# Layer 2's queries projected straight into transposed form, two units at a time

## The chip, the cores and the metric

The kernel runs on one NeuronCore of a Trainium2 chip. Its engines work at the same time, each through its own list of instructions in program order, and meet by semaphores: TensorE (PE, matrix products; PEld is its loading of weights), VectorE (DVE), ScalarE (ACT), GpSimd (POOL) and SyncE (SP, which issues transfers). PE writes into PSUM, from where DVE and ACT take results to SBUF. The metric is the time of one execution on the device, in microseconds (us).

## The reference, cut to what matters

The input x is two batches of 1024 rows of 256 numbers. Four layers follow, each added to x: two attention layers and two mixtures of experts. The second attention layer, the one that is changed, is:

```python
xn = layernorm(x, g_in)
q = (xn @ Wq).reshape(b, n, H, DH).transpose(0, 2, 1, 3) * scale
kv = xn @ Wkv
k, v = (kv[..., :DH], kv[..., DH:])
...
sim = jnp.einsum('bhid,bjd->bhij', q, k)
sim = sim + bias
...
sim = jnp.where(causal_mask, neg, sim)
sim = jnp.where(mask_p[:, None, None, :], sim, neg)
attn = jax.nn.softmax(sim, axis=-1)
out = jnp.einsum('bhij,bjd->bhid', attn, v)
out = out.transpose(0, 2, 1, 3).reshape(b, n, INNER)
out = out @ Wo
return layernorm(out, g_out)
```

There are H = 16 heads of DH = 64, one key and value for all heads, and a null key and value in front. The first attention layer also normalizes each query and key row to length 1; the second does not.

## The kernel before

Attention goes over tiles of 128 query rows (8 a layer), and in a tile over 8 *units*: 4 groups of 4 heads, times 2 batches. A unit u has 4 *steps*, one per head. N = 512 steps n are written out in one list for both layers, m, k = divmod(n, 4). The tile number sets how many keys a step has (causal): 128 in a layer's first tile, 1024 in its last.

In step n, each engine has a fixed order of work that belongs to different units and steps:

- PE: the scores of step n + 3 (lines 1347 and 1348, queries stationary, keys moving); at k = 0 the output product y of unit m - 2; at k = 3 the transposes of the queries of unit m + 2 (line 1371); at k = 1 the projection of the queries of unit m + 3 (rows of x stationary, wq moving); then the transposes of the probabilities of step n (line 1456) and the product with the values of step n - 1. A function `small()` in the middle of a step holds the rest: for a new tile the transposes of x (xt, 15 steps ahead), keys and values (11 and 7 steps ahead); at k = 0 the null score of unit m + 1, at k = 2 the transposes of the attention output (o_n, line 1444).
- ACT: the exponential of step n + 1 (probs, line 673); at k = 0 the eviction of y (line 687); at k = 3 the evictions of the transposed queries to q_b (line 694, one for each of two halves of partitions) and a copy of q_b to q_a (line 698); at k = 1 the eviction of the projected queries to q_n (line 707); then p_hi of step n (line 765).
- DVE: at k = 1 the output of a unit (o_raw, r_den); the score pass of step n + 2 (line 994, which adds the bias, applies the mask and keeps the row's extreme); at k = 3 the rest of the queries to q_a (line 1022, two halves); then p_lo of step n (line 1078), with ot_lo (line 1068) or neg_null behind it at k = 2 and k = 0.

Numbers that PE multiplies are kept as a sum of two 16-bit halves, hi and lo, so each product is three (`three`, lines 1157 to 1159), and the queries stand in q_b (upper 64 partitions a constant for the mask, lower the hi half) and q_a (hi and lo), transposed, with two slots by u % 2. Each wait is written by hand, as in ACT's part at k = 3:

```python
act.wait_ge(s["q_t"], u + 1)
if u >= 2:
    act.wait_ge(s["scores"], HU * (u - 1))
```

PSUM has 8 banks: four for scores, two for transposed probabilities (tp), one for the output (op) and one, aux, for all else. While tiles have up to 512 keys, halves of the score banks are free, and `banks(n)` gives them to y and to `small()`; in wider tiles everything uses aux, and `take` makes PE wait until the last user of the bank has been read.

Of the kernel before, what the change touches and what calls it, by code (L numbers as in the profile page):

```python
# [28 lines left out]
P = 128  # L29
# [5 lines left out]
HU = 4  # L35
# [56 lines left out]
def model(nc, a, out):  # L92
# [3 lines left out]
    with ctx:  # L96
# [26 lines left out]
        q_n = sb("q_n", [P, 2, UW])  # L123
        q_sq = sb("q_sq", [P, HU, DH])
# [49 lines left out]
        ones64 = sb("ones64", [G, P])  # L174
# [72 lines left out]
        def sems(part, names):  # L247
# [8 lines left out]
                    q_proj q_sq q_ss q_nd q_na q_t q_hi q_lo q_dup q_null null  # L256
# [160 lines left out]
        def _(pool):  # L417
# [29 lines left out]
            gp.memset(q_b[DH:P, :, :], BIG).then_inc(setup["big"], 1)  # L447

# [4 lines left out]
            pool.wait_ge(setup["big"], 1)  # L453
# [140 lines left out]
        def _(act):  # L594
# [63 lines left out]
            for n in range(FIRST, LAST):  # L658
# [29 lines left out]
                if k == 3 and 0 <= m + 2 < NU:  # L688
# [10 lines left out]
                if k == 1 and 0 <= m + 3 < NU:  # L699
                    u = m + 3  # L700
                    act.wait_ge(s["q_proj"], u + 1)
                    if u < U0:
                        if u >= 1:
                            act.wait_ge(s["q_ss"], u)
                        ac.activation(q_sq[:, :, :].rearrange("p h d -> p (h d)"), first[:, 0:UW], ACT.Square)\
                            .then_inc(s["q_sq"], 1)
                    ac.activation(q_n[:, u % 2, :], first[:, 0:UW], ACT.Copy, scale=1.0 if u < U0 else DH ** -0.5 / WS)\
                        .then_inc(s["q_na"], 1)

                def small():  # L710

                    for T in range(STEPS):
                        n0 = T * STEP_N
                        layer, t = divmod(T, TILES)
                        if n == n0 - 15:
                            act.wait_ge(s["xt"], T + 1)
                            if T >= 2:
                                act.wait_ge(s["q_proj"], UNITS * (T - 1))
# [77 lines left out]
        def _(dve):  # L796
# [167 lines left out]
            for n in range(FIRST, LAST):  # L964
# [53 lines left out]
                if k == 3 and 0 <= m + 2 < NU:  # L1018
# [133 lines left out]
        def _(pe):  # L1152
# [165 lines left out]
            for n in range(FIRST, LAST):  # L1318
# [6 lines left out]
                if 0 <= i < N:  # L1325
# [6 lines left out]
                    if h == 0:  # L1332
                        pe.wait_ge(s["q_dup"], u + 1)
                        pe.wait_ge(s["q_lo"], 2 * (u + 1))
# [9 lines left out]
                    for c0 in range(0, w, 512):  # L1344
                        cw = min(512, w - c0)
                        o_ = sc[i % 2][:, c0:c0 + cw]
                        te.matmul(o_, q_a[:, u % 2, cols], k_a[layer][:, bt, c0:c0 + cw], start=True, stop=False)  # L1347
                        last = te.matmul(o_, q_b[:, u % 2, cols], k_b[layer][:, bt, c0:c0 + cw],  # L1348
# [15 lines left out]
                if k == 3 and 0 <= m + 2 < NU:  # L1364
# [3 lines left out]
                    if u < U0:  # L1368
                        pe.wait_ge(s["q_nd"], u + 1)
# [3 lines left out]
                if k == 1 and 0 <= m + 3 < NU:  # L1373
                    u = m + 3
                    layer = u // U0
                    T, hg, bt = u // UNITS, (u % UNITS) // B, u % B
                    take(False, (s["q_na"], u + 1), (s["q_sq"], min(u + 1, U0)))
                    if hg == 0:
                        if layer == 0:
                            pe.wait_ge(s["xr_lo"], T + 1)  # L1380
                        pe.wait_ge(s["xt_lo"], T + 1)
                        if T % TILES == 0:
                            pe.wait_ge(job_done, job_end[3 * layer + 1])
                    for kc in range(KC):
                        cols = slice(hg * UW, (hg + 1) * UW)
                        x_q = xr if layer == 0 else xt[:, T % 2]
                        last = three(first[:, 0:UW], x_q[:, 0, bt, kc, :], x_q[:, 1, bt, kc, :],
                                     wq[layer][:, 0, kc, cols], wq[layer][:, 1, kc, cols],
                                     kc == 0, kc == KC - 1)
                    last.then_inc(s["q_proj"], 1)  # L1390

                def small():
# [31 lines left out]
                    if k == 0 and 0 <= m + 1 < NU:  # L1424
# [4 lines left out]
                        pe.wait_ge(s["q_lo"], 2 * (u + 1))  # L1429
                        if u == 0:  # L1430
                            pe.wait_ge(setup["big"], 1)
# [66 lines left out]
```

## Time and profile before

| What | us |
|---|---|
| median of 3 runs | 1704.15 |
| their range | 1701.85 to 1704.22 |
| the profiled execution | 1700.64 |
| its span, first to last instruction | 1698.8 |

The profile is that of one execution; its span is the time from its first to its last instruction, and 1.8 us of the execution lie around it. Layer 1's steps go from 88.6 us to 740.8, layer 2's to about 1352, and the two mixtures of experts follow. A unit of queries is the same work in both layers, but for the normalization in layer 1 (a squaring on ACT, a sum on DVE, and a scaling on POOL).

### The profile page before, as it was taken

The page shows a single profiled execution, that of the slowest core. Times are in us where ns is not written, and L with a number is a line of the kernel's source. Part 1 is how long each engine was busy: PE and PEld are TensorE (multiplying, and loading weights), DVE is VectorE, ACT ScalarE, POOL GpSimd, SP SyncE. Part 2 cuts the span into 40 slices and gives each one's busy share as a digit, 9 for nine tenths or more (in the row PEclk, how much of TensorE's full clock was granted, in tenths as well). Part 3 has the DMA queues.
Part 4 walks back from the last instruction along what each step waited for, and adds up shares of the span by engine and source line. Part 5 has one row for each costly group of instructions (what it writes and reads, how often), then busy time and mean ns, then how long its engine had stood idle before and what let it go on. Part 6 is the DMA issues. An engine that isn't in the chain of part 4 may idle for free.

```text
span 1698.8 us, 46470 instructions
## 1 busy us (share of the span) xinstructions
PE 1458.5 (86%) x16377; PEld 1076.6 (63%) x16377; DVE 1415.3 (83%) x3651; ACT 1210.4 (71%) x3064; POOL 750.8 (44%) x1412
## 2 busy tenths in 40 slices
PE   1467778888889999987788888999999989999998
PEld 1245556666667777765666666677777756666665
DVE  4557778888898999987788888899999979888886
ACT  1268778888889989988888888889999923333332
POOL 5657776543433434356665332323212156632222
PEclk9679999999999999999999999999999999999999
DMA  4002121211122213111221211222123001000000
GB/s 140 5 27 63 52 63 51 81 65 43 66 76 88 88 51 126 57 39 32 70 76 58 76 64 70 76 82 71 63 101 131 22 1 43 2 1 1 14 14 26
DMA packets 50504, 96.70 MB, mean 57 GB/s; under 512 B 3396, under 2 KB 27092, under 8 KB 50276
## 3 DMA queue, kind: packets, MB, share of 16 engines
q1 hardware_dynamic: 45568, 90.27, 16.1%
q10 hardware_dynamic: 4708, 3.45, 0.7%
q8 instruction: 135, 2.21, 0.5%
q14 instruction: 93, 0.76, 0.1%
HBM read 91.54 MB, written 2.17 MB: 55 GB/s over the span
## 4 chain that ended last, share of the span: by engine, by line
PE 46%; DVE 18%; ACT 14%; issue 10%; POOL 3%; DMA 1%; DVEq 0%; ACTq 0%; POOLq 0%; SPq 0%
PE tp L1456 7%; DVE p_lo L1078 7%; ACT p_hi L765 6%; DVE biased L994 5%; PE sc L1159 4%; PE sc L1157 4%; PE sc L1158 4%; PE sc L1347 3%; ACT q_b L694 3%; PE sc L1348 3%; ACT probs L673 3%; PE op L1157 2%; PE aux L1157 2%; PE tp L1157 2%; PE tp L1159 2%
## 5 line engine op out<-in xcount | busy, mean ns | idle before, releaser
L1078 DVE TENSOR_TENSOR p_lo<-tp,p_hi 128x512 f16<-128x512 f32 (+3 forms) x768 | 416.7, 554 | 119.1 <-ACT p_hi L765 112.2
L994 DVE CUSTOM_DVE_ANT_0 biased<-sc,bias,neg_null 128x256 f32<-128x256 f32 (+7 forms) x512 | 411.2, 803 | 2.7 <-issue 0.8
L673 ACT ACTIVATE probs<-biased,neg_max 128x256 f32<-128x256 f32 (+7 forms) x512 | 395.7, 773 | 14.4 <-DVE neg_max L994 12.8
L1456 PE MATMUL tp<-ident,probs 128*128 128x128 f32 x2304 | 388.6, 278 | 17.5 <-DVE p_lo L1078 15.5
L765 ACT ACTIVATE p_hi<-tp 128x512 f16<-128x512 f32 (+3 forms) x768 | 368.9, 491 | 43.0 <-PE tp L1456 32.8
L1157 PE MATMUL op<-v_s,p_hi 128*128 128x64 f16 x2304 | 284.9, 194 | 53.9 <-DVE p_lo L1078 35.2
L1347 PE MATMUL sc<-k_a,q_a 128*128 128x512 f16 (+3 forms) x768 | 254.4, 331 | 67.0 <-DVE neg_max L994 59.9
L1456 PEld LDWEIGHTS tp<-ident,probs 128*128 128x128 f32 x2304 | 267.9, 142 | 52.3 <-issue 37.6
L1158 PE MATMUL op<-v_s,p_hi 128*128 128x64 f16 x2304 | 284.0, 194 | 0.0
L1159 PE MATMUL op<-v_s,p_lo 128*128 128x64 f16 x2304 | 284.0, 194 | 0.0
L1157 PEld LDWEIGHTS op<-v_s,p_hi 128*128 128x128 f16 x2304 | 215.8, 99 | 85.9 <-DVE p_lo L1078 62.2
L1348 PE MATMUL sc<-k_b,q_b 128*128 128x512 f16 (+3 forms) x768 | 242.0, 329 | 0.0
L1158 PEld LDWEIGHTS op<-v_s,p_hi 128*128 128x128 f16 x2304 | 210.2, 98 | 7.4
L1159 PEld LDWEIGHTS op<-v_s,p_lo 128*128 128x128 f16 x2304 | 210.5, 98 | 0.0
L477 POOL TENSOR_TENSOR p_lo<-probs,p_hi 128x512 f16<-128x512 f32 x80 | 92.5, 1156 | 176.2 <-ACT p_hi L650 176.2
L529 POOL TENSOR_TENSOR denom<-rows,p_null 128x4 f32<-128x4 f32 x128 | 25.6, 200 | 325.0 <-ACT p_null L774 325.0
L1347 PEld LDWEIGHTS sc<-k_a,q_a 128*128 128x128 f16 x768 | 75.2, 98 | 130.2 <-DVE neg_max L994 89.5
L497 POOL TENSOR_TENSOR o_n<-o_raw,r_den 128x256 f32<-128x256 f32 x128 | 78.4, 613 | 147.1 <-DVE o_raw L973 145.9
L650 ACT ACTIVATE p_hi<-probs 128x512 f16<-128x512 f32 x80 | 50.4, 630 | 130.5 <-DVE probs L926 130.5
L1022 DVE TENSOR_TENSOR q_a<-aux,q_b 64x256 f16<-64x256 f32 x256 | 108.1, 422 | 27.7 <-ACT q_b L694 20.0
L644 ACT ACTIVATE biased<-sc 128x512 f32<-128x512 f32 x80 | 47.7, 596 | 90.5 <-PE sc L1159 90.5
L694 ACT ACTIVATE q_b<-aux 64x256 f16<-64x256 f32 x256 | 96.5, 377 | 20.5 <-PE aux L1371 14.5
(268 smaller groups left out, 3609.7 us busy)
## 6 DMA issues: line engine op xcount, KB each, us to landing
bias<-rel_table SPq DMA_DIRECT2D x4, 2048.0 KB, 8.4
bias<-in_fside_16xSxS SPq DMA_DIRECT2D x4, 2048.0 KB, 8.0
bias<-rel_table SPq DMA_DIRECT2D x4, 1792.0 KB, 8.1
bias<-in_fside_16xSxS SPq DMA_DIRECT2D x4, 1792.0 KB, 7.1
bias<-rel_table SPq DMA_DIRECT2D x4, 1536.0 KB, 6.1
bias<-in_fside_16xSxS SPq DMA_DIRECT2D x4, 1536.0 KB, 6.6
bias<-rel_table SPq DMA_DIRECT2D x4, 1280.0 KB, 6.1
bias<-in_fside_16xSxS SPq DMA_DIRECT2D x4, 1280.0 KB, 5.6
```

The source lines that it names most:

```text
L673: ac.activation(probs[:, i % 2, 0:w], biased[:, i % 2, 0:w], ACT.Exp, bias=neg_max[:, u % 2, i % HU:i % HU + 1], scale=-1.0, accum_out=row ...
L694: ac.activation(heads(q_b[0:DH, u % 2, :], e), first[e * DH:(e + 1) * DH, 0:UW].rearrange("p (c q) -> p c q", q=P), ACT.Copy)\
L765: ac.activation(p_hi[:, gi % 4, 0:nb * P], tp[gi % 2][:, 0:nb * P], ACT.Copy)\
L994: ve.tensor_tensor_reduce(out=biased[:, i % 2, 0:w], in0=sc[i % 2][:, 0:w], in1=bias[:, g % 2, i % HU, 0:w], scale=-1.0, scalar=neg_null[: ...
L1022: ve.tensor_tensor(heads(q_a[DH:P, u % 2, :], e), first[e * DH:(e + 1) * DH, 0:UW].rearrange("p (c q) -> p c q", q=P), heads(q_b[0:DH, u % ...
L1078: ve.tensor_tensor(p_lo[:, gi % 4, 0:nb * P], tp[gi % 2][:, 0:nb * P], p_hi[:, gi % 4, 0:nb * P], ALU.subtract).then_inc(s["p_lo"], 1)
L1157: te.matmul(out_, l_hi, r_hi, start=first, stop=False)
L1158: te.matmul(out_, l_hi, r_lo, start=False, stop=False)
L1159: return te.matmul(out_, l_lo, r_hi, start=False, stop=last)
L1347: te.matmul(o_, q_a[:, u % 2, cols], k_a[layer][:, bt, c0:c0 + cw], start=True, stop=False)
L1348: last = te.matmul(o_, q_b[:, u % 2, cols], k_b[layer][:, bt, c0:c0 + cw], start=False, stop=True)
L1456: last = te.transpose(tp[gi % 2][:, jj * P:(jj + 1) * P], probs[:, n % 2, (j0 + jj) * P:(j0 + jj + 1) * P], ident[:, :])
```

## The change

For layer 2's units (u from U0 = 64 on) the projection is turned round: wq is stationary and x, for both batches, is moving, so the product comes out transposed, for two units at once (the same heads of both batches). It is done in the even unit's step k = 1, for units m + 2 and m + 3; ACT takes hi of both units to q_b in two instructions, DVE forms lo of both in two, and ACT's copies of hi to q_a follow at k = 2 and k = 3, one for each unit. Row-wise queries (q_n) and their transposes are gone there, and at k = 3 and in odd units at k = 1 the old work is left out. Queries get a second pair of buffers: q_a2 is the memory of q_n, q_b2 is new, and POOL fills its constant half in the set-up; for room, some small tiles of the set-up move into the memory of biased. Layer 1 works as before.

```diff
+        def q_pair(u):
+
+            return (q_a2, q_b2) if u // 2 % 2 == 0 else (q_a, q_b)
...
+        def q_parts(u):
+
+            return 2 * (u + 1) if u < NU // 2 else 2 * (u // 2 * 2 + 2)
...
+            gp.memset(q_b2[DH:P, :, :], BIG).then_inc(setup["big"], 1)
...
+                if k == 1 and U0 <= m + 2 < NU and m % 2 == 0:
+                    u = m + 2
+                    act.wait_ge(s["q_dir"], (u - U0) // 2 + 1)
+                    act.wait_ge(s["scores"], HU * (u - 2))
+                    for e in range(2):
+                        ac.activation(pair_heads(q_pair(u)[1][0:DH, :, :], e), pair_in(first, e), ACT.Copy,
+                                      scale=DH ** -0.5 / WS).then_inc(s["q_hi"], 2)
+                if k >= 2 and U0 <= m + 2 < NU and m % 2 == 0:
+                    u = m + k
+                    act.wait_ge(s["q_hi"], q_parts(u))
...
+                    ac.activation(q_of(u)[0][0:DH, :], q_of(u)[1][0:DH, :], ACT.Copy).then_inc(s["q_dup"], 1)
-                if k == 3 and 0 <= m + 2 < NU:
+                if k == 3 and 0 <= m + 2 < U0:
...
+                if k == 1 and U0 <= m + 2 < NU and m % 2 == 0:
+                    u = m + 2
+                    dve.wait_ge(s["q_hi"], q_parts(u))
...
+                    for e in range(2):
+                        ve.scalar_tensor_tensor(pair_heads(q_pair(u)[0][DH:P, :, :], e), pair_in(first, e),
+                                                DH ** -0.5 / WS, pair_heads(q_pair(u)[1][0:DH, :, :], e),
+                                                ALU.mult, ALU.subtract).then_inc(s["q_lo"], 2)
-                if k == 3 and 0 <= m + 2 < NU:
+                if k == 3 and 0 <= m + 2 < U0:
...
+                if k == 1 and U0 <= m + 2 < NU and m % 2 == 0:
                     u = m + 2
-                    take(False, (s["q_lo"], 2 * (u + 1)))
+                    T, hg = u // UNITS, (u % UNITS) // B
+                    take(False, (s["q_lo"], q_parts(u)))
...
+                    for c in range(UW // P):
+                        cols = slice(hg * UW + c * P, hg * UW + (c + 1) * P)
+                        for kc in range(KC):
+                            last = three(first.rearrange("p (b c q) -> p c b q", b=B, q=P)[:, c],
+                                         wq[1][:, 0, kc, cols], wq[1][:, 1, kc, cols],
+                                         xt[:, T % 2, 0, :, kc, :], xt[:, T % 2, 1, :, kc, :],
+                                         kc == 0, kc == KC - 1)
+                    last.then_inc(s["q_dir"], 1)
+                if k == 3 and 0 <= m + 2 < U0:
```

How the instructions stand on ACT, in layer 2's tile of 512 keys: before, from a unit's step k = 1 to its step k = 3 (a step begins with probs; q_n is the row-wise eviction, q_b and q_a the transposed queries).

```order
L673 ACTIVATE probs,rows<-biased,neg_max 128x512
L707 ACTIVATE q_n<-aux 128x256
L765 ACTIVATE p_hi<-tp 128x512
L673 ACTIVATE probs,rows<-biased,neg_max 128x512
L765 ACTIVATE p_hi<-tp 128x512
L754 ACTIVATE ot_hi<-sc 128x256
L673 ACTIVATE probs,rows<-biased,neg_max 128x512
L694 ACTIVATE q_b<-aux 64x2x128 x2
L698 ACTIVATE q_a<-q_b 64x512
L765 ACTIVATE p_hi<-tp 128x512
```

The same steps of an even unit after the change (here the buffer of q_a lies in the memory of q_n, and has its name).

```order
L697 ACTIVATE probs,rows<-biased,neg_max 128x512
L717 ACTIVATE q_b<-aux 64x4x128 x2
L802 ACTIVATE p_hi<-tp 128x512
L697 ACTIVATE probs,rows<-biased,neg_max 128x512
L724 ACTIVATE q_n<-q_b 64x512
L802 ACTIVATE p_hi<-tp 128x512
L791 ACTIVATE ot_hi<-sc 128x256
L697 ACTIVATE probs,rows<-biased,neg_max 128x512
L724 ACTIVATE q_n<-q_b 64x512
L802 ACTIVATE p_hi<-tp 128x512
```

The evictions of the transposed queries, now of 512 columns, have moved from k = 3 to k = 1, and one copy stands ahead of p_hi at k = 2 and at k = 3. In an odd unit none of these rows is there.

On DVE, the same tile, before: the steps k = 2 and k = 3 of a unit (a score pass is two rows, ISA).

```order
L994 ISA biased,neg_max<-sc,bias,neg_null 128x512
L994 ISA neg_max 128x1
L1078 TENSOR_TENSOR p_lo<-tp,p_hi 128x512
L1068 TENSOR_TENSOR ot_lo<-sc,ot_hi 128x256
L994 ISA biased,neg_max<-sc,bias,neg_null 128x512
L994 ISA neg_max 128x1
L1022 TENSOR_TENSOR q_a<-aux,q_b 64x2x128 x2
L1078 TENSOR_TENSOR p_lo<-tp,p_hi 128x512
```

After the change, from the step k = 1 of an even unit to its step k = 3.

```order
L1031 ISA biased,neg_max<-sc,bias,neg_null 128x512
L1031 ISA neg_max 128x1
L1061 SCALAR_TENSOR_TENSOR q_n<-aux,q_b 64x4x128 x2
L1124 TENSOR_TENSOR p_lo<-tp,p_hi 128x512
L1031 ISA biased,neg_max<-sc,bias,neg_null 128x512
L1031 ISA neg_max 128x1
L1124 TENSOR_TENSOR p_lo<-tp,p_hi 128x512
L1114 TENSOR_TENSOR ot_lo<-sc,ot_hi 128x256
L1031 ISA biased,neg_max<-sc,bias,neg_null 128x512
L1031 ISA neg_max 128x1
L1124 TENSOR_TENSOR p_lo<-tp,p_hi 128x512
```

The two subtractions have moved from k = 3 to k = 1 and have twice the columns; at k = 3 nothing stands between the score pass and p_lo.

## Rows read from the trace of the kernel before

**Rows 1.** the page, part 1: each engine, busy us (share), instructions.

```profile
PE 1458.5 (86%) x16377; PEld 1076.6 (63%) x16377; DVE 1415.3 (83%) x3651; ACT 1210.4 (71%) x3064; POOL 750.8 (44%) x1412
```

**Rows 2.** windows, two tiles of layer 2: busy us, instructions; clock, DMA share, GB/s.

```profile
915.90:987.70 71.80, 62.65 (x781) 47.88 (x780) 61.10 (x161) 61.55 (x159) 25.18 (x54) 1.00 0.22 68
...
1256.50:1345.00 88.50, 86.43 (x1184) 68.61 (x1183) 84.31 (x164) 80.93 (x164) 20.95 (x45) 1.00 0.28 96
```

**Rows 3.** DVE in time, a unit of 512 keys: start, us, instruction, [idle].

```profile
938.09 0.74 DVE L994 CUSTOM_DVE_ANT_0 biased<-sc,bias,neg_null 128x512 f32<-128x512 f32 x1
...
940.13 0.72 DVE L994 CUSTOM_DVE_ANT_0 biased<-sc,bias,neg_null 128x512 f32<-128x512 f32 x1
...
941.95 0.74 DVE L994 CUSTOM_DVE_ANT_0 biased<-sc,bias,neg_null 128x512 f32<-128x512 f32 x1
...
943.66 0.74 DVE L994 CUSTOM_DVE_ANT_0 biased<-sc,bias,neg_null 128x512 f32<-128x512 f32 x1
...
944.68 0.88 DVE L1022 TENSOR_TENSOR q_a<-aux,q_b 64x256 f16<-64x256 f32 x2 [0.28 <-ACT q_b L694]
945.97 0.69 DVE L1078 TENSOR_TENSOR p_lo<-tp,p_hi 128x512 f16<-128x512 f32 x1 [0.41 <-ACT p_hi L765]
946.58 0.74 DVE L994 CUSTOM_DVE_ANT_0 biased<-sc,bias,neg_null 128x512 f32<-128x512 f32 x1
```

**Rows 4.** ACT in time, the same unit, its step k = 3 on.

```profile
943.89 0.77 ACT L694 ACTIVATE q_b<-aux 64x256 f16<-64x256 f32 x2
944.68 0.63 ACT L698 ACTIVATE q_a<-q_b 64x512 f16<-64x512 f16 x1
945.34 0.60 ACT L765 ACTIVATE p_hi<-tp 128x512 f16<-128x512 f32 x1
...
946.63 0.37 ACT L687 ACTIVATE y_acc<-sc 128x256 f32<-128x256 f32 x1
```

**Rows 5.** PE in time, the same unit, its step k = 1.

```profile
938.99 0.38 PE L1347 MATMUL sc<-k_a,q_a 128*128 128x512 f16 x1
...
939.42 0.27 PE L1157 MATMUL aux<-wq,xt 128*128 128x256 f16 x1
...
939.96 0.27 PE L1159 MATMUL aux<-wq,xt 128*128 128x256 f16 x1
940.07 0.60 PE L1456 MATMUL tp<-ident,probs 128*128 128x128 f32 x4
```

**Rows 6.** instructions by form, layer 2: count, busy us, mean ns, idle before.

```profile
L1078 DVE TENSOR_TENSOR p_lo<-tp,p_hi 128x512 f16<-128x512 f32 x185 | 126.8, 689 | 34.4 <-ACT p_hi L765 32.4
L765 ACT ACTIVATE p_hi<-tp 128x512 f16<-128x512 f32 x186 | 110.3, 597 | 14.9 <-PE tp L1456 11.2
...
L1022 DVE TENSOR_TENSOR q_a<-aux,q_b 64x256 f16<-64x256 f32 x126 | 53.2, 422 | 12.2 <-ACT q_b L694 8.4
...
L694 ACT ACTIVATE q_b<-aux 64x256 f16<-64x256 f32 x126 | 47.4, 376 | 7.7 <-PE aux L1371 5.1
...
L1371 PE MATMUL aux<-ident,q_n 128*128 128x128 f32 x126 | 26.0, 289 | 3.9 <-DVE ot_lo L1068 3.3
...
L707 ACT ACTIVATE q_n<-aux 128x256 f32<-128x256 f32 x61 | 23.4, 384 | 27.4 <-PE aux L1159 26.7
```

**Rows 7.** waits of PE, us 1000 to 1340: us, times, longest.

```profile
PEld aux L1157 <- DVE q_a L1022: 10.8, 29, 1.2
PEld aux L1371 <- DVE ot_lo L1068: 10.3, 26, 0.6
```

**Rows 8.** line 994 over a 768-key tile, layer 1, then layer 2.

```profile
L994 DVE CUSTOM_DVE_ANT_0 biased<-sc,bias,neg_null x32: 981/1007/1019, 446.4 to 536.7; 128x768 f32<-128x768 f32 x32
...
L994 DVE CUSTOM_DVE_ANT_0 biased<-sc,bias,neg_null x32: 981/1007/1018, 1074.0 to 1160.7; 128x768 f32<-128x768 f32 x32
```

**Rows 9.** POOL in time, the start of the kernel.

```profile
19.89 0.95 POOL L447 MEMSET q_b<- 64x1024 f16 x1
...
55.42 0.28 POOL L440 TENSOR_SCALAR r_rs<-r_mv 128x8 f32<-128x8 f32 x1 [9.45 <-DVE r_mv L834]
```

More of the change, by code:

```diff
@@ L698, in _ @@
                     ac.activation(q_a[0:DH, u % 2, :], q_b[0:DH, u % 2, :], ACT.Copy).then_inc(s["q_dup"], 1)
-                if k == 1 and 0 <= m + 3 < NU:
+                if k == 1 and 0 <= m + 3 < U0:
                     u = m + 3
                     act.wait_ge(s["q_proj"], u + 1)
[L702 to L708, printed above, removed]
+                    if u >= 1:
+                        act.wait_ge(s["q_ss"], u)
+                    ac.activation(q_sq[:, :, :].rearrange("p h d -> p (h d)"), first[:, 0:UW], ACT.Square)\
+                        .then_inc(s["q_sq"], 1)
+                    ac.activation(q_n[:, u % 2, :], first[:, 0:UW], ACT.Copy).then_inc(s["q_na"], 1)
                 def small():
@@ L1346, in _ @@
                         o_ = sc[i % 2][:, c0:c0 + cw]
-                        te.matmul(o_, q_a[:, u % 2, cols], k_a[layer][:, bt, c0:c0 + cw], start=True, stop=False)
-                        last = te.matmul(o_, q_b[:, u % 2, cols], k_b[layer][:, bt, c0:c0 + cw],
+                        te.matmul(o_, q_of(u)[0][:, cols], k_a[layer][:, bt, c0:c0 + cw], start=True, stop=False)
+                        last = te.matmul(o_, q_of(u)[1][:, cols], k_b[layer][:, bt, c0:c0 + cw],
                                          start=False, stop=True)
@@ L1428, in small @@
                         pe.wait_ge(s["q_dup"], u + 1)
-                        pe.wait_ge(s["q_lo"], 2 * (u + 1))
+                        pe.wait_ge(s["q_lo"], q_parts(u))
                         if u == 0:
-                            pe.wait_ge(setup["big"], 1)
+                            pe.wait_ge(setup["big"], 2)
                         for h in range(HU):
                             cols = slice(h * P, (h + 1) * P)
-                            te.matmul(second[:, h:h + 1], q_a[:, u % 2, cols], kn_a[:, layer:layer + 1], start=True, stop=False)
-                            last = te.matmul(second[:, h:h + 1], q_b[:, u % 2, cols], kn_b[:, layer:layer + 1],
+                            te.matmul(second[:, h:h + 1], q_of(u)[0][:, cols], kn_a[:, layer:layer + 1], start=True, stop=False)
+                            last = te.matmul(second[:, h:h + 1], q_of(u)[1][:, cols], kn_b[:, layer:layer + 1],
                                              start=False, stop=True)
```

60 lines of the change are left out of this document (37 added, 23 removed).

## The prediction

> **What bounds it now.** The page's first part gives no single bound: PE is busy 86% of the span, DVE 83%, ACT 71% [rows 1]. So I read the windows tile by tile. In layer 2 no engine is full alone: in the tile of 512 keys ACT is busy 61.55 of 71.8 us, DVE 61.10, PE 62.65; in the tile of 1024 keys PE 86.43, DVE 84.31 and ACT 80.93 of 88.5 [rows 2]. PE's clock is at its upper level there (1.00). So I looked at the order in time of one unit of 512 keys. DVE's four score passes begin at 938.09, 940.13, 941.95, 943.66, and the next unit's at 946.58 [rows 3]: steps of 2.04, 1.82, 1.71 and 2.92 us, 8.49 for the unit. The reader is to see the long one, the step k = 3: DVE idles 0.28 us for q_b, subtracts for 0.88, idles 0.41 for p_hi, because ACT runs the two q_b (0.77) and q_a (0.63) ahead of p_hi [rows 3, 4]. Engines work in program order, so a query instruction that waits holds up the probabilities behind it. The step time is that chain across engines more than anyone's busy time.
>
> **The change, part by part.** A name for the steps of a pair of units: e0 to e3 for the even unit, o0 to o3 for the odd one.
>
> *PE.* Per unit, the projection stays six products of 256 columns; they start 0.108 us apart (939.42 to 939.96, five gaps) [rows 5], 0.65 a unit. Now twelve come at once in e1, 1.30 us, none in o1. The two transposes of a unit go: line 1371's group is busy 26.0 us for 63 units, 0.41 each, of which 0.17 is the last one's landing and can overlap; some 0.2 us of PE's time a unit, 15 us in all [rows 6].
>
> *ACT.* Before, a unit has one q_n (0.384), two q_b (0.376 each) and one q_a (0.63) [rows 4, 6], 1.77 us. After, a pair has two q_b of 64x512 and two q_a. The new q_b form isn't in the trace. From below, twice the 64x256 with nothing fixed saved is 0.75; from the other side, line 765 with the same 512 columns from PSUM takes 0.597 [rows 6], and I take that: the row differs in partitions alone. Both q_b of a pair take 0.77, more than 2 x 0.376 [rows 4]: the second does not overlap the first. So the new pair costs 2 x 0.60 + 0.03 = 1.23, and ACT spends (1.23 + 1.26)/2 = 1.25 us a unit: 0.52 saved, 33 us over 64 units.
>
> *DVE.* Two subtractions of 64x256 (0.88 together) become, per pair, two fused ones of 64x512; bounds 0.689 (line 1078, same columns and sources) and 0.84 (twice 0.422) [rows 3, 6]. I take 0.69, 1.41 for the two: 0.70 a unit, 0.18 saved, 11 us in all.
>
> *Waits removed and added.* In tiles above 512 keys everything small shares one PSUM bank, aux. There the y product waits for q_a (10.8 us in 340) and the transposes wait for ot_lo (10.3) [rows 7]; both go. Added: in e1 DVE waits for both q_b, behind it stand p_lo and the next score pass, and for p_lo waits PE's op product. Two of ACT's q_a stand in e2 and e3, ahead of p_hi; nothing waits for them until the next unit, but p_hi is 0.63 later.
>
> *Set-up.* One more memset of 0.95 on POOL is hidden in POOL's later idle stretch of 9.45 us [rows 9]; without that cover it costs 0.95. Small tiles moved into biased add no instruction.
>
> *The pair of 512 keys, worked through.* I lay the new order out by hand with the durations above, each instruction starting when its engine and its sources are free.
> - e1, score pass to score pass: PE takes 0.43 for scores (939.42 - 938.99), 1.30 for q, 0.17 until the last lands (0.27 - 0.11) [rows 5]; then ACT 1.23, DVE 1.41, p_lo 0.61 (946.58 - 945.97) [rows 3], and 0.03 at two hand-overs: 5.2 us in a row. PE, held up by y, starts this 1.35 us before the first of the two passes, so the step is 3.85 us (before 1.82), and DVE idles 1.1 of it.
> - o1 has no query work: 1.29 (before 1.82).
> - k = 3: e3 keeps one q_a, 2.17; o3 has nothing, 1.28 (before 2.92 each).
> - k = 2: 1.67 in e2; 2.25 in o2, where the o transposes now come last (before 1.71).
> - k = 0: 2.17 in o0, 3.00 in e0 (before 2.04). The short o3 lets e0's pass begin early, and then y (0.65 on PE, 0.37 on ACT [rows 4]) ends last.
>
> Sum 17.68 a pair against 2 x 8.49 = 16.98: +0.70 us. The same layout with the shorter rows gives +1.1 at 256 keys (I take it for 128 too, 0.9 for 384). At 640 the removed waits on aux outweigh the chain, -0.55; at 768 +0.1, at 1024 +0.3, where PE, nearly full, runs during most of DVE's wait. These are estimates, good to perhaps 0.4 each; 896 gets 0.2. Sum over the eight tile sizes: 1.1 + 1.1 + 0.9 + 0.7 - 0.55 + 0.1 + 0.2 + 0.3 = 3.85, times four pairs a tile: +15.4 us.
> - Once a tile, the transposes of xt and of k stand in e1. Above 512 keys they use aux, so PE waits for q_lo: 2 x 3 times about 0.5, +3. Against it, waits that the first unit of each tile has for the row statistics lie behind e1's chain, 8 x -0.5 = -4.
>
> So +14.4 us: 1700.64 + 14.4 = 1715 in terms of the profiled execution. That one was 3.5 us under the median of its runs (1704.15) and below all three; I set the forecast between the two bases, 1717.
>
> **A rule against the trace.** The Trainium skill, Perfetto Trace Analysis, section Optimizing Scalar/DVE Operations, says two things that part here. Grouping into larger operations raises throughput if the engine is saturated; if the engines are not saturated but make bubbles on others, breaking instructions up lets work finish sooner. By the first, ACT's 33 us would come back, some 1670; by the second, this change goes the wrong way. The rows [rows 2, 3] show DVE idle and waiting with ACT at 86% in the tile of 512 keys, which is nearer to the second.
>
> **The rivals.**
> - *Faster: the time follows busy time.* For it speaks layer 1, whose units do the same with one more squaring on ACT and one more sum on DVE. A tile of 768 keys takes 90.3 us there from first to last score pass, and 86.7 in layer 2 [rows 8]; taking work off both engines gave 0.45 us a unit. The change takes 0.52 off ACT, 0.18 off DVE, 0.2 off PE. If the odd unit and the early q_a make good e1's chain, 0.12 to 0.5 a unit returns, 64 units: 8 to 32 us, 1671 to 1695. Against it, e1's chain stands in program order on all three engines, and the odd unit can't take its steps before. It decides from the point where DVE's wait in e1 falls from the 1.1 us that I work out to some 0.4. The grouping sentence of the Trainium skill, Perfetto Trace Analysis, would have it so.
> - *No change:* the narrow tiles lose the 15 us and the wide ones win as much by the waits on aux [rows 7]: 1703 within 3.
> - *Slower still:* the chain shows in the wide tiles too, 0.7 a pair there as well; 16 pairs at 0.7 in place of about 0 is +11, and each stall on aux 1 us in place of 0.5 is +3: 1731. Against it, DVE in the 1024-key tile has 84.3 us of work in 88.5 to do meanwhile [rows 2].
>
> **How the numbers follow.** Chances: the forecast 0.52, slower still 0.15, faster 0.23, no change 0.10. Apart from no change by 0.2% (3.4 us, about what a measurement of this kernel can tell) that makes faster 0.23, same 0.10, slower 0.67. The likeliest case's own range is 1708 to 1727: 0.4 us either way on about half of the 32 pairs is 6, and the longer bounds of the new forms (0.75 and 0.84 in place of 0.60 and 0.69) add 0.6 a pair in the 16 narrow pairs, 10 us. As cases of both signs hold much of the chance, the range reaches from 1690, in the faster case, to 1733.
>
> **What would show it.** Line 717's q_b near 0.60 each and line 1061's q_n/q_a near 0.69; no transposes of q_n in layer 2; in tiles up to 512 keys a wait of DVE for q_b of about 1 us once in eight steps, followed by a score pass 3.5 us or more after the last; short steps near 1.3 us in odd units; in tiles above 512 keys no wait of y for q_a, and layer 1 as it was. I am wrong if tiles up to 512 keys are not longer, if the new forms take half of what I put, or if the odd unit's slack takes the chain in.

## The result, and the profile after

| | before | after |
|---|---|---|
| median, us | 1703.86 | 1738.97 |
| range, us | 1701.85 to 1704.22 | 1736.39 to 1740.08 |
| profiled execution, us | 1700.64 | 1736.39 |
| its span, us | 1698.8 | 1734.6 |

The changed kernel is slower by 2.1%: ratio 1.0208, 95% interval 1.0194 to 1.0221. That is 35 us where 13 were forecast, and above the range's upper end of 1733.

The page's first part, to be read against [rows 1]: PE, DVE and ACT are busy 4, 14 and 26 us less than before, PEld and POOL 4 and 2 us more, and the span is 36 us longer. So most of what came is waiting; the rest is PE's work at a lower clock, shown next.

```profile
PE 1454.4 (84%) x16249; PEld 1081.0 (62%) x16249; DVE 1401.1 (81%) x3587; ACT 1184.2 (68%) x2936; POOL 752.8 (43%) x1413
```

The windows of layer 2, one row for each tile from 128 to 1024 keys, cut at a tile's first score pass (busy us of PE, PEld, DVE, ACT, POOL; then PE's granted clock, DMA share, GB/s); they answer to [rows 2].

```profile
745.10:807.90 62.80, 42.77 (x461) 33.65 (x460) 37.01 (x154) 38.73 (x144) 34.31 (x74) 0.79 0.15 39
807.90:868.70 60.80, 44.06 (x504) 35.30 (x504) 42.83 (x152) 43.69 (x142) 36.01 (x77) 0.91 0.22 58
868.70:938.10 69.40, 55.08 (x633) 43.16 (x632) 50.68 (x152) 51.21 (x142) 36.62 (x78) 0.90 0.22 62
938.10:1013.80 75.70, 60.76 (x769) 47.26 (x767) 59.03 (x152) 58.62 (x143) 25.81 (x55) 0.98 0.19 61
1013.80:1101.30 87.50, 74.21 (x948) 58.60 (x947) 69.94 (x182) 67.94 (x171) 24.49 (x52) 0.96 0.18 64
1101.30:1193.20 91.90, 80.41 (x1082) 64.34 (x1081) 78.09 (x185) 75.07 (x174) 24.53 (x52) 1.00 0.21 73
1193.20:1292.60 99.40, 89.91 (x1209) 72.73 (x1208) 86.97 (x184) 82.38 (x174) 24.51 (x52) 0.98 0.22 79
1292.60:1389.80 97.20, 91.05 (x1262) 73.30 (x1260) 88.51 (x168) 84.58 (x162) 22.44 (x48) 1.00 0.26 88
```

The same windows of before, the tiles of 128 and 384 keys; from 256 keys on all of before's tiles have the clock at 1.00.

```profile
740.80:796.10 55.30, 40.88 (x478) 31.89 (x476) 38.71 (x163) 42.57 (x162) 34.09 (x73) 0.91 0.17 45
...
852.70:915.90 63.20, 53.29 (x649) 41.54 (x648) 52.71 (x160) 54.15 (x159) 36.45 (x77) 1.00 0.24 68
```

The reader is to see two things. In the tile of 384 keys DVE's work fell by 2.0 us and ACT's by 2.9, and the tile is 6.2 us longer. And the last column but two: PE's granted clock is 0.90 there, 0.79 in the tile of 128 keys. The two levels are 1.2 and 2.4 GHz, so 0.90 over 69.4 us is 2 x 0.10 x 69.4 = 13.9 us at the lower one. Over layer 2 that makes some 65 us, against 10 before. The forecast has no word on this.

The new forms, grouped over layer 2 (they answer to [rows 6]):

```profile
L717 ACT ACTIVATE q_b<-aux 64x512 f16<-64x512 f32 x62 | 36.8, 594 | 35.4 <-issue 34.7
...
L1061 DVE SCALAR_TENSOR_TENSOR q_a<-aux,q_b 64x512 f16<-64x512 f32 x32 | 22.0, 689 | 18.0 <-ACT q_b L717 17.5
L1061 DVE SCALAR_TENSOR_TENSOR q_n<-aux,q_b 64x512 f16<-64x512 f32 x30 | 20.7, 689 | 22.9 <-ACT q_b L717 22.4
```

0.594 and 0.689 us each, the values I took (0.60, 0.69). The idle time in front is the chain: ACT stands 35.4 us for the products (the profile names no releaser), DVE 39.9 us for q_b, over 31 pairs.

Now e1 of a pair of 512 keys in time. DVE first, as in [rows 3]:

```profile
963.64 0.72 DVE L1031 CUSTOM_DVE_ANT_0 biased<-sc,bias,neg_null 128x512 f32<-128x512 f32 x1
...
965.58 1.41 DVE L1061 SCALAR_TENSOR_TENSOR q_n<-aux,q_b 64x512 f16<-64x512 f32 x2 [1.20 <-ACT q_b L717]
967.01 0.69 DVE L1124 TENSOR_TENSOR p_lo<-tp,p_hi 128x512 f16<-128x512 f32 x1
967.62 0.74 DVE L1031 CUSTOM_DVE_ANT_0 biased<-sc,bias,neg_null 128x512 f32<-128x512 f32 x1
...
969.34 0.74 DVE L1031 CUSTOM_DVE_ANT_0 biased<-sc,bias,neg_null 128x512 f32<-128x512 f32 x1
...
971.34 0.74 DVE L1031 CUSTOM_DVE_ANT_0 biased<-sc,bias,neg_null 128x512 f32<-128x512 f32 x1
```

Score pass to score pass 3.98, 1.72, 2.00 us; I had laid out 3.85, 1.67, 2.17, with DVE idle for 1.1 (1.20 here). In the tile's other three pairs e1 took 4.94, 4.04 and 4.32 us. ACT in the same step, as in [rows 4]:

```profile
964.26 1.21 ACT L717 ACTIVATE q_b<-aux 64x512 f16<-64x512 f32 x2 [1.04 <-issue]
965.50 0.60 ACT L802 ACTIVATE p_hi<-tp 128x512 f16<-128x512 f32 x1
```

And PE, behind its query products and the scores and transposes that follow them:

```profile
965.23 0.60 PE L1512 MATMUL tp<-ident,probs 128*128 128x128 f32 x4
967.76 0.20 PE L1203 MATMUL op<-v_s,p_hi 128*128 128x64 f16 x1 [1.93 <-DVE p_lo L1124]
...
968.43 0.39 PE L1393 MATMUL sc<-k_a,q_a 128*128 128x512 f16 x1
968.66 0.55 PE L1394 MATMUL sc<-k_b,q_b 128*128 128x512 f16 x1
969.00 1.06 PE L1512 MATMUL tp<-ident,probs 128*128 128x128 f32 x4
...
970.52 0.61 PE L1393 MATMUL sc<-k_a,q_a 128*128 128x512 f16 x1
...
971.35 0.42 PE L1203 MATMUL sc<-wo,ot_hi 128*128 128x256 f16 x1
```

PE stands still for 1.93 us, until p_lo; 0.9 us later its instructions take longer: four transposes 1.06 in place of 0.60, a score product 0.61 in place of 0.38, a product of y 0.42 in place of 0.27. That is the lower clock, and PE does its work of e3 and the first part of o0's under it. Score pass to score pass, o0 took 3.42 us here (2.17 laid out) and 2.94, 2.62 and 2.50 in the tile's other pairs, without the lower clock. PE stood for p_lo in those pairs too, 2.29, 1.46 and 1.68 us; so the lower clock does not follow every such wait, and not even the longest.

PE's waits in the tiles above 512 keys (us in all, times, longest), after:

```profile
PE tp L1512 <- DVE p_lo L1124: 13.2, 16, 2.1
PE sc L1393 <- DVE neg_max L1031: 6.7, 22, 0.4
PE aux L1478 <- DVE q_n L1061: 6.6, 3, 2.4
PE aux L1459 <- DVE q_a L1061: 6.2, 3, 2.1
PE tp L1512 <- ACT probs L697: 3.6, 3, 1.2
```

and the largest of before in its tiles:

```profile
PE tp L1456 <- DVE p_lo L1078: 7.3, 22, 0.4
PE aux L1157 <- DVE q_a L1022: 4.2, 10, 0.9
PE aux L1371 <- DVE ot_lo L1068: 3.0, 10, 0.4
```

y's wait for q_a and the transposes' wait for ot_lo are gone, as forecast. In their place PE waits for p_lo up to 2.1 us at a time (0.4 before; 0.8 on average, 0.3 before), and the transposes of k (line 1478) and of xt (line 1459) wait for the queries' subtraction, six times, 2.1 us each.

Layer 1 is as it was but for its last tile, where layer 2's first products run: 104.8 us after, 102.7 before. Its first score pass comes at 91.1 us (88.6 before).

### The profile page after: what moved, and what is told of

Its sections match the earlier page's. It is cut to its first block, busy times and chain, and to the rows that moved or that the text cites. A ratio compares the mean times of both kernels' runs of the same rounds, so it can differ in the third digit from the quotient of the medians.

```text
span 1734.6 us, 45947 instructions
## 1 busy us (share of the span) xinstructions
PE 1454.4 (84%) x16249; PEld 1081.0 (62%) x16249; DVE 1401.1 (81%) x3587; ACT 1184.2 (68%) x2936; POOL 752.8 (43%) x1413
## 3 DMA queue, kind: packets, MB, share of 16 engines
q8 instruction: 133, 2.18, 0.5%
HBM read 91.54 MB, written 2.17 MB: 54 GB/s over the span
## 4 chain that ended last, share of the span: by engine, by line
PE 46%; DVE 23%; issue 11%; ACT 10%; POOL 2%; DVEq 1%; ACTq 0%; POOLq 0%
DVE biased L1031 7%; PE tp L1512 7%; DVE p_lo L1124 6%; PE sc L1203 4%; PE sc L1205 4%; ACT p_hi L802 4%; PE sc L1204 4%; PE sc L1393 4%; PE sc L1394 3%; PE tp L1203 2%; PE tp L1205 2%; PE tp L1204 2%; PE aux L1203 2%; PE op L1203 2%; ACT q_b L731 2%
## 5 line engine op out<-in xcount | busy, mean ns | idle before, releaser
L1512 PE MATMUL tp<-ident,probs 128*128 128x128 f32 x2304 | 394.4, 281 | 26.3 <-DVE p_lo L1124 21.0
L1512 PEld LDWEIGHTS tp<-ident,probs 128*128 128x128 f32 x2304 | 273.7, 144 | 66.5 <-issue 25.9
L1394 PE MATMUL sc<-k_b,q_b 128*128 128x512 f16 (+3 forms) x768 | 246.0, 334 | 0.0
L1393 PE MATMUL sc<-k_a,q_a 128*128 128x512 f16 (+3 forms) x576 | 193.3, 336 | 57.1 <-DVE neg_max L1031 52.3
L1393 PEld LDWEIGHTS sc<-k_a,q_a 128*128 128x128 f16 x576 | 56.8, 99 | 106.1 <-DVE neg_max L1031 76.6
L951 DVE SCALAR_TENSOR_TENSOR x<-tp,comb,x 128x256 f32<-128x256 f32 x256 | 105.6, 473 | 0.0
L697 ACT ACTIVATION_READ_ACCUMULATOR probs<-biased,neg_max 128x1 f32 x512 | 100.6, 197 | 0.0
```

Source lines behind the costliest of these rows:

```text
L697: ac.activation(probs[:, i % 2, 0:w], biased[:, i % 2, 0:w], ACT.Exp, bias=neg_max[:, u % 2, i % HU:i % HU + 1], scale=-1.0, accum_out=row ...
L951: ve.scalar_tensor_tensor(x_t, tp[i // 2][:, (i % 2) * D:(i % 2 + 1) * D], weight, x_t, ALU.mult, ALU.add).then_inc(f["y"], 1)
L1393: te.matmul(o_, q_of(u)[0][:, cols], k_a[layer][:, bt, c0:c0 + cw], start=True, stop=False)
L1394: last = te.matmul(o_, q_of(u)[1][:, cols], k_b[layer][:, bt, c0:c0 + cw], start=False, stop=True)
L1512: last = te.transpose(tp[gi % 2][:, jj * P:(jj + 1) * P], probs[:, n % 2, (j0 + jj) * P:(j0 + jj + 1) * P], ident[:, :])
```

## The experiments

Medians are against the kernel before, run on the same chip. That kernel took 1703.86 us beside the changed kernel and 1700.5 to 1701.4 beside the experiments, so I compare an experiment with the changed kernel by their ratios, not by their medians. The theory that I began with (A): e1's chain, products, q_b, subtraction, stands in program order in the way of the probabilities, and its length is the loss. The rivals come up as they are needed.

### Query work behind the probabilities, and half by half

e1_behind puts ACT's and DVE's query instructions of e1 behind the first group's p_hi and p_lo:

```diff
-                if k == 1 and U0 <= m + 2 < NU and m % 2 == 0:
+                def queries():
...
                     if j == 0:
+                        queries()
                         small()
```

Expected: 

> In e1, ACT's two q_b and DVE's two subtractions stand behind the first group's p_hi and p_lo instead of ahead of them; nothing else changes. Theory A (the chain of product, q_b and subtraction stands in program order ahead of the probabilities, and PE waits for p_lo behind it): PE's wait of p_lo in e2 falls from about 2 us to under 1, the clock is granted more fully in the tiles up to 512 keys because PE no longer stands still there, and 0.7 to 1.3 us a pair come back: 32 pairs, 22 to 42 us, so 1697 to 1717. Rival C (it is the amount of query work gathered in one step that costs, wherever it stands in the step): within 8 us of the changed kernel, 1731 to 1747.

Measured: 1748.22 us, ratio 1.028 (1.0263 to 1.0297), some 12 us slower than the changed kernel (1.0208). Theory A had it the other way round. PE's waits in its tile of 512 keys, then those of the changed kernel's:

```profile
PE sc L1399 <- DVE neg_max L1034: 13.3, 16, 2.6
```

```profile
PE op L1203 <- DVE p_lo L1124: 7.4, 4, 2.3
PE sc L1393 <- DVE neg_max L1031: 5.5, 15, 0.6
```

The wait for p_lo is gone, and the one for the score pass has taken its place (5.5 to 13.3). The subtractions now stand between p_lo and the next score pass, and PE can't write the scores of a later step before that pass has read its tile. So taking the work from ahead of the probabilities doesn't give the loss back: DVE is held for 1.2 + 1.4 us inside one step, and PE has not enough ahead to last that long.

e2_halves lets DVE start with the first q_b:

```diff
-                    dve.wait_ge(s["q_hi"], q_parts(u))
...
                     for e in range(2):
+                        dve.wait_ge(s["q_hi"], q_parts(u) - 2 + 2 * e)
```

Expected: 

> DVE waits for q_b half by half, so its first subtraction starts when the first q_b is done, 0.6 us sooner; all else as in the changed kernel. Theory A: e1 is a chain in a row, so 0.6 us less in it is up to 0.6 a pair, 32 pairs, and 10 to 19 us come back: 1720 to 1729. Rival D (not the chain's length in e1 but TensorE's lower clock after any standstill sets the loss): PE still stands still for over a us in each e1, the low stretches remain, and the time stays within 5 us of 1739.

Measured: 1710.44 us, 1.0049 (1.0034 to 1.0064): some 27 us back, more than the 19 that the chain's 0.6 us gives. The tiles tell why (table below): the tile of 1024 keys is 1.8 us shorter, three pairs of 0.6, but that of 384 keys 6.0, and there the clock is back (a window that begins 1.2 us behind the tile's first score pass):

```profile
866.00:929.00 63.00, 49.17 (x633) 39.10 (x632) 50.78 (x151) 50.03 (x141) 36.16 (x76) 1.00 0.24 69
```

### The subtraction left out

e4_no_lo cuts the subtraction to one column a handle:

```diff
+                        n_ = P if u < U0 + 4 else 1
-                        ve.scalar_tensor_tensor(pair_heads(q_pair(u)[0][DH:P, :, :], e), pair_in(first, e),
+                        ve.scalar_tensor_tensor(pair_heads(q_pair(u)[0][DH:P, :, :], e)[:, :, 0:n_], pair_in(first, e)[:, :, 0:n_],
```

Expected: 

> Leaves out most of DVE's subtraction: from the third pair on each of the two handles one column of 128, so lo of the queries is missing. DVE's part of the chain falls from 1.41 to about 0.3 us a pair. Theory A: p_lo then waits only for p_hi, some 0.9 us sooner in e1, and 0.9 to 1.4 a pair come back, 29 to 45 us: 1694 to 1710. Rival E (ACT's q_b and q_a ahead of p_hi hold the probabilities up, DVE has slack): less than 12 us, 1727 to 1739.

Measured: 1702.25 us, 1.0003 (0.9994 to 1.0013). Some 35 us came back for the 30 pairs that have the edit, 1.2 each with what the clock gave back, where DVE's part got some 1.1 shorter. So what DVE does in e1 goes into the time nearly one for one, in the wide tiles too: 3.7 us for four pairs in that of 768 keys, whose clock was 1.00 with and without it. ACT's copies ahead of p_hi, which this run keeps, are not the cause.

### The clock

Is the lower clock a cause of lost time, or only a sign that PE waits? e3_filler and e5_filler2 add products that nobody reads, where PE stands still in e2:

```diff
+                    if j == 0 and k == 2 and m % 2 == 0 and U0 <= m + 2 < NU and free_banks(n):
+                        release(0)
+                        free[0] = ()
+                        for _ in range(6):
+                            te.matmul(sc[0][:, 512:1024], wq[1][:, 0, 1, 0:P], wq[1][:, 0, 0, 0:512],
+                                      start=True, stop=True)
                     if j < len(before):
                         pv(before[j])
```

(e3 has eight, with bank 1 in place of 0.) Expected of e3: 

> Adds eight products of 512 columns to PE in step e2 of each pair in layer 2's tiles up to 512 keys, into a bank that nobody reads, at the place where PE otherwise waits for p_lo; nothing is taken away. In the changed kernel the clock is granted at 0.50 for 64.7 us of layer 2, against 10.2 before, and 0.79 to 0.91 on average in the first three tiles. Rival D (the lower clock is a good part of the loss beyond the forecast): the low stretches in these tiles go, and 8 to 20 us come back, 1719 to 1731. Theory A alone (PE is not on the path while it has the lower clock): the clock rises and the time stays within 4 us of 1739, or rises by what the products delay.

Measured: 1749.58 us, 1.0292 (1.0267 to 1.0318), slower. My edit added a wait: that bank also holds the transposes of xt and k, and PE now stood until DVE had read them, up to 2.8 us at a time and 17.9 us in all in these tiles, which are 20 us longer. It tells nothing on the clock. Of e5: 

> The changed kernel with six products of 512 columns added to PE in step e2 of each pair in the tiles up to 512 keys, now into the unused half of the score bank that the o transposes take next, so that PE waits for nothing new (in the run before, it waited at that place for the transposes of x and k to be read). Six take about 1.3 us at the upper clock, less than PE's standstill there. Rival D (the lower clock costs a good part of the miss): the low stretches of the tiles of 256 to 512 keys (10.2, 13.7 and 3.4 us) mostly go, and with them 5 to 12 us: 1727 to 1734. Theory A alone: the clock rises, the time stays within 4 us of 1739.

Measured: 1727.09 us, 1.0156 (1.0141 to 1.0171): 96 idle products more in 16 pairs, and some 9 us less. Its tiles of 128 to 512 keys:

```profile
741.90:802.20 60.30, 44.61 (x485) 33.36 (x484) 37.03 (x154) 38.53 (x144) 34.27 (x74) 0.86 0.17 41
802.20:862.40 60.20, 46.47 (x528) 35.73 (x528) 42.60 (x152) 43.10 (x142) 36.06 (x77) 0.97 0.21 59
862.40:928.10 65.70, 54.75 (x657) 41.61 (x656) 50.71 (x152) 50.62 (x142) 36.54 (x78) 1.00 0.23 66
928.10:1002.60 74.50, 64.41 (x793) 48.56 (x791) 59.02 (x152) 58.41 (x143) 25.83 (x55) 1.00 0.21 62
```

At 384 keys: 69.40 at 0.90 became 65.70 at 1.00. PE did more instructions (657 for 633) in less time. Over the four tiles 268.7 us fell to 260.7, and the time at 1.2 GHz from 54 to 20.5 us (2 x (1 - clock) x length, summed): about 0.24 us lost for each us at the lower clock. The Trainium skill, TensorE: Matmul & The Clock Gate, section HAM oscillation — how this bites in real kernels, counts half of the time at the lower clock as lost in its example. Here it is less, 0.24; PE was not busy all the time anyway (55.1 of 69.4 us at 384 keys).

The rate is rough: tile by tile it is 0.26, 0.08, 0.27 and 0.40. Two tiles that the filler leaves as they were bear it out. That of 768 keys had clock 0.96 in e5 and 1.00 in the changed kernel, 7.5 us at 1.2 GHz, and took 93.5 us against 91.8; that of 640 keys had 0.98 against 0.96, and took 86.5 against 87.5. So with the same instructions a us at the lower clock cost 0.23 and 0.29. What else the two profiles differ by is not the filler's: 2.7 us lie before the first score pass.

The same tiles let the chain be read alone, if the added products cost nothing where PE stood: at 384 and 512 keys, with the clock at 1.00, e5 is 2.5 and 2.7 us above before; forecast 3.6 and 2.8.

### Query work spread over steps

e6_split makes the pair's product in two halves of the columns, six in o1 of the pair before and six in e1:

```diff
+        def q_slot(m):
+
+            u = m // 2 * 2 + 2 + 2 * (m % 2)
...
+            return u, (0,) if m % 2 else (1,)
...
-                    for e in range(2):
-                        ac.activation(pair_heads(q_pair(u)[1][0:DH, :, :], e), pair_in(first, e), ACT.Copy,
+                    for c in cs:
...
+                        for e in range(2):
+                            ac.activation(half_heads(q_pair(u)[1][0:DH, :, :], c, e), half_in(first, c, e), ACT.Copy,
```

Expected: 

> The pair's transposed queries in two halves: six products in o1 of the pair before and six in e1, each followed by ACT's two q_b of 64x256 and DVE's two subtractions of 64x256 in the same step. No row-wise queries and no transposes, as in the changed kernel, but the old forms (0.376 and 0.42 each). Theory A (a chain is dear by its length within one step): the chain is 0.65 + 0.17 + 0.77 + 0.88 = 2.5 us in each of two steps in place of 4.0 in one; ACT has still 0.38 us a unit less than before the change, PE 0.2 less; 1690 to 1712. Rival C (gathering at k = 1, ahead of the probabilities, is what costs, and twice as often costs as much): 1730 to 1745.

Measured: 1705.47 us, 1.0038 (1.0024 to 1.0052). Expected of e7_split_behind, the same with `queries()` as in e1_behind: 

> As the run in halves of the columns, with ACT's and DVE's query instructions behind the first group's p_hi and p_lo. By what e1_behind showed (the next score pass is held up wherever the subtractions stand in the step, and the bank aux is given back later), 0 to 10 us slower than the same in front; if the chain of 2.5 us fits behind the probabilities while PE still has two score tiles ahead, up to 10 us faster than it.

Measured: 1723.72 us, 1.0137 (1.0122 to 1.0152), 18 us slower than in front: worse than expected, but the same sign as e1_behind. What comes behind p_lo holds the score pass up and gives aux back later. In the tiles of 640 to 896 keys PE's wait for the pass rose from 5.4 us (e6) to 12.4, its waits on aux for the subtractions from 9.4 to 17.7.

e8_spread, which has e2's edit too, leaves the forms of 512 columns, and does the second q_b and its subtraction in e3, in tiles up to 512 keys:

```diff
-                if k == 1 and U0 <= m + 2 < NU and m % 2 == 0:
+                if k % 2 == 1 and U0 <= m + 2 < NU and m % 2 == 0:
...
+                    for e in ((k // 2,) if spread(m) else range(2) if k == 1 else ()):
```

Expected: 

> On top of e2_halves (DVE waits half by half, 1710.4): in tiles up to 512 keys the second half of the heads is evicted and subtracted in e3 instead of e1, and ACT's two q_a stand in e3 and o1. Aux has no other user there. Theory A: the subtractions are 0.69 us in each of two steps, the wait for q_b falls to some 0.5 us in e1 alone; 1 to 2 us a tile and pair of those 16 come back over halves: 1695 to 1706. Rival D (the low clock of the narrow tiles, 47.8 us in e2_halves, decides there and comes from the units without query work): 1706 to 1712.

Measured: 1701.73 us, 1.0009 (1.0000 to 1.0019), level with before, with the same instructions as e2_halves. Together with e2 and e6: the loss isn't the new forms, it is the length of the chain in one step of eight. Most of it, some 27 of 35 us, came back already when DVE no longer waited for the second q_b before it began (e2), with all the work still in e1. What e8 adds to that came in the narrow tiles alone (256.4 to 247.9 us in four; in the wide ones its edit changes nothing). The Trainium skill, Perfetto Trace Analysis, section Optimizing Scalar/DVE Operations, says that breaking up instructions may let work end sooner where Scalar/Vector aren't saturated but cause bubbles on other engines. These runs agree: some 29 us between the changed kernel and e6_split.

### The transposes that wait for aux

e9_moved moves layer 2's transposes of xt and k from e1 to e3:

```diff
-                        if n == n0 - 15:
+                        if n == n0 - (13 if layer else 15):
...
-                        if n == n0 - 7:
+                        if n == n0 - (5 if layer else 7):
```

Expected: 

> The changed kernel with layer 2's transposes of xt and of k, with all that belongs to them on ACT and DVE, moved from e1 to e3 (two steps later); queries as in the changed kernel. In the tiles of 640 to 896 keys PE waits six times for the subtraction of the queries before these transposes, 12.8 us in all, where the forecast put some 0.5 us each, 3 in all. Theory F (these stalls are the term that was mis-sized in the wide tiles): they go, and 8 to 12 us come back, 1727 to 1731. Rival: the transposes only meet another user of aux, or their own evictions hold p_hi and p_lo up in e3 as they did in e1; under 4 us, 1735 to 1739.

Measured: 1741.54 us, 1.0241 (1.0224 to 1.0259): theory F, by which the stalls on aux are what was mis-sized in the wide tiles, falls. The waits on aux are gone, but PE's wait for p_lo in the tiles of 640 to 896 keys is 23.4 us, 12.9 before the move:

```profile
PE tp L1512 <- DVE p_lo L1124: 23.4, 19, 2.2
```

These three tiles got 3.1 us shorter together, the narrow ones 12.8 longer: there PE's products now wait 7.5 us for the readers of xt and k, and 77 us are at the lower clock, not 54 (the profiled execution was 4.8 us above the run's median). So the stalls on aux were for the most part e1's chain seen at another instruction. Expected of e10_spread_moved: 

> e8_spread (1701.7) with the same move of the transposes of xt and k from e1 to e3 in layer 2. Theory F with what the runs so far show: the stalls in the wide tiles are some 0.6 shorter there, so 5 to 9 us come back, 1692 to 1697, below the kernel before the change by 0.2 to 0.5%. If the chain in the wide tiles and not these stalls is what is left: 1699 to 1703.

Measured: 1716.52 us, 1.0089 (1.0074 to 1.0104). Of e11_filler_moved: 

> The changed kernel with both: PE's six added products in e2 in the tiles up to 512 keys (e5_filler2, 1727.1), and the transposes of xt and k in e3. The query chain itself is as in the changed kernel. If the miss of the forecast is the lower clock and the stalls on aux, and the chain was sized rightly, then with both away the time comes to the forecast's 1717, within 5 us: 1712 to 1722. If the chain was mis-sized too, it stays above 1722.

Measured: 1736.52 us, 1.0208 (1.0191 to 1.0225). Both missed for the same reason, the move's harm in the narrow tiles; e11 doesn't test the chain's size, as I had meant it to. It does test the filler a second time: beside e9 on the same chip, with nothing else changed, it is 5.0 us faster, and in the profiles the narrow tiles fell by 9.3 us with 47.6 us less at the lower clock, 0.20 for each.

### The chain begun earlier

e12_swap has PE issue e1's query products ahead of that step's scores (the block is moved up unchanged). Expected: 

> The changed kernel with PE's twelve query products in e1 issued ahead of that step's score products instead of behind them; nothing else. The chain then begins earlier by the time of the scores, some 0.2 us at 128 keys, 0.4 at 512 and 0.9 at 1024. Theory A for the wide tiles too (the chain's length goes into the time one for one, as 0.6 us less did in e2_halves): 0.5 to 0.9 a pair in the wide tiles and 0.1 to 0.4 in the narrow ones, 10 to 16 us in all: 1723 to 1729. Rival G (in the wide tiles PE is nearly full, and the scores put back cost there what the queries win): within 4 us of 1739 in all, with tiles above 512 keys no shorter.

Measured: 1723.81 us, 1.0127 (1.0113 to 1.0141), as theory A had it in sum, though not in each tile: 1.6 us back at 1024 keys, nothing at 768. PE's waits from 1019 to 1279 us, most of its tiles of 640 to 896 keys, show why:

```profile
PE tp L1512 <- DVE p_lo L1124: 8.2, 16, 1.6
PE aux L1203 <- DVE neg_null L1107: 6.8, 11, 1.0
```

the products, now early, wait for DVE to read the null scores out of aux (1.4 us in the changed kernel). Expected of e13_spread_swap: 

> e8_spread (1701.7) with the same swap. Theory A: the wide tiles become 2 to 3.5 us shorter each, the narrow ones little, so 8 to 13 us: 1689 to 1694, 0.4 to 0.7% faster than the kernel before the change. Rival G: 1699 to 1704.

Measured: 1700.64 us, 0.9999 (0.9990 to 1.0008); theory A failed, and the rival had it right. The wide tiles gave 1.3 us in all, as there the products wait for the null scores again (7.6 us). Of e14_spread_swap_mw: 

> e13 with the transposes of xt and k moved from e1 to e3 in tiles from 640 keys on only (in e9 and e10 these tiles got 0.5 to 2.6 us shorter by it, the narrow ones 1.3 to 6 longer). 1 to 3 us under e13; if the stalls on aux are only the chain seen in another place, and the swap has already shortened it, within 1 us.

Measured: 1697.82 us, 0.9978 (0.9968 to 0.9987): 0.2% faster than before, the only version here that is.

Tile lengths in us, from the profiles, cut as the windows above (low: us at 1.2 GHz in layer 2):

| keys | 128 | 256 | 384 | 512 | 640 | 768 | 896 | 1024 | low |
|---|---|---|---|---|---|---|---|---|---|
| before | 55.3 | 56.6 | 63.2 | 71.8 | 86.3 | 89.1 | 93.5 | 95.7 | 10 |
| after | 62.8 | 60.8 | 69.4 | 75.7 | 87.5 | 91.8 | 99.4 | 97.2 | 65 |
| e2_halves | 61.6 | 59.5 | 63.4 | 71.9 | 83.5 | 89.2 | 95.8 | 95.4 | 48 |
| e4_no_lo | 60.1 | 56.3 | 62.7 | 71.8 | 82.1 | 88.1 | 94.7 | 95.0 | 31 |
| e5_filler2 | 60.3 | 60.2 | 65.7 | 74.5 | 86.5 | 93.5 | 99.4 | 97.2 | 34 |
| e6_split | 57.9 | 56.1 | 62.4 | 70.6 | 84.5 | 89.5 | 96.6 | 94.9 | 21 |
| e8_spread | 56.9 | 58.1 | 62.3 | 70.6 | 83.4 | 89.1 | 95.8 | 95.4 | 21 |
| e12_swap | 62.4 | 61.6 | 65.5 | 72.6 | 85.9 | 91.9 | 97.5 | 95.6 | 48 |
| e14_spread_swap_mw | 56.6 | 60.6 | 61.3 | 69.4 | 83.4 | 88.4 | 93.7 | 94.6 | 31 |

## Why the prediction was right in sign and wrong in size

- **Prices of the forms:** right. 0.594 and 0.689 as taken; the pair of q_b 1.21 (1.23). In busy time ACT saved 26 us, DVE 14 and PE 4, where I had 33, 11 and 15; PE's includes 55 us more at the lower clock.
- **The mechanism:** right in what I looked for, but for the short steps. DVE waits for q_b once in eight steps, a score pass comes 3.98 us after the last, y no longer waits for q_a. In the tile of 512 keys o3 is short twice (1.27; once 2.19), but o1 in one pair of four (1.24; 1.95, 2.18 and 2.24 in the others, where I laid out 1.29). Taking 1.1 us out of that chain (e4), beginning it by halves (e2) or cutting it up (e6, e8) gives all or most of the loss back.
- **The chain up to 512 keys:** oversized if anything. I had +15.2 us. Measured +21.8, of which the lower clock is some 10.6 (44 us more of it, at 0.24), so about 11 for the chain. That the sum came out near is in part luck: e1, o0 and o1 were longer than laid out, e3 shorter.
- **The clock:** the step that failed most. The prediction read it in before ("at its upper level there (1.00)") and did not ask whether it would stay there when PE stands still for 2 us in e1; its sum has no term for it. Over layer 2 it is 55 us more at 1.2 GHz, at 0.24 about 13 us.
- **"PE, nearly full, runs during most of DVE's wait":** wrong. I had -0.55, +0.1, +0.2 and +0.3 a pair at 640 to 1024 keys, 0.2 us in all; measured +11.3. PE stands for p_lo up to 2.1 us at a time, and every tenth of the chain counts (e2: 2.6 us for 2.4 at 768 keys). The clock's share here is some 2.6 (11 us more of it at 0.24), which leaves 8 to 9. Only the tile of 1024 keys, from which I judged, came out as laid out (+1.5, forecast +1.2). The waits on aux that went were worth little, and I had read the wrong rows for them: the 10.8 and 10.3 us of [rows 7] are waits of PEld, the loading of weights. PE's own two waits were 4.2 and 3.0 us in all of the wide tiles (the list of before above).
- **Stalls of xt and k:** put at 0.5 us each, seen as 2.1 each, 12.8 in all; but e9 shows that most of it is the chain again, and only 3 us came back when the transposes were moved out of it. The -4 for hidden waits on row statistics wasn't measured by itself.
- **Not in the forecast:** the tile in which layer 2's first products run, +2.1. The start, +2.5, isn't shown to be the change's: kernels with the changed set-up reached the first score pass at 88.4 (e5) to 91.4 us (e8), before in its one profile at 88.6. The memset took 1.09 us on POOL, which later idled 10.95 us in one piece.

Sum, in terms of the profiled executions: 11 + 8.5 + 13 + 2.1 + 2.5, less 1.8 at the end of the kernel, 35.3; measured 35.75. That it closes proves little, as both terms of the chain are what the clock's term leaves of the tiles. The rival "slower still" (the chain shows in the wide tiles too, 1731) described the wide tiles better than my forecast did, and the clock came on top. The split between clock and chain rests on that one rate, and is good to a few us. It is a split of one cause, too: where the chain was shortened (e2, e4, e6, e8), the lower clock went with it in all tiles but the first two. In the tile of 128 keys, long in most runs with low clock, the two were not separated.

## What to carry to other kernels

Grouping small instructions saves busy time, but what it gathers into one step can't be longer than the other engines can run ahead: here PE has two score tiles, and a chain of 4 us in one step of eight costs more than 26 us of saved ACT time give; the same work in two steps is level with before. Look first at what the chain waits for: letting DVE begin with the first of two results, a wait moved by one line, gave some 27 of the 35 us back. When a change makes PE wait longer at one place, ask in the forecast what its clock will be after that wait, and price it by rows at both clocks. A wait that disappears from the table of waits is a gain only if the next instruction doesn't wait for the same chain: e1_behind and e9_moved both moved a wait without shortening it.

## What the runs showed of the hardware that was not expected

In the pair of 512 keys shown above, PE worked, stood still for 1.93 us, worked on for 0.9, and then had the lower clock. That is common here, but not the rule. In the changed kernel's tiles up to 512 keys PE stands for p_lo once in each of 16 pairs, 1.26 to 2.91 us long. Read in stretches of 0.5 us, the granted clock was at its lower level at most some 2 us after the end of eleven of these waits; after the other five (1.46, 1.50, 1.68, 2.24 and 2.29 us) it stayed at 1.00. So the length of the wait alone doesn't tell whether the clock falls, and what does is left open by these runs. In e2_halves, whose longest wait for p_lo in the tile of 512 keys is 1.3 us, the clock was at 1.00 throughout that tile.

96 products whose result nobody reads made the kernel some 9 us faster, with 54 us at the lower clock reduced to 20.5 in the four tiles that have them; in e11, beside e9, they gave 5 us.
